# A graph network's row gathers, released five select pairs sooner

## The reference

```
gat(x):  h = x @ W                       # 4 heads of 32
         e = leaky(a_src[src] + a_dst[dst]); ex = exp(e - max over dst)
         out[dst] = sum(ex * h[src]) / sum(ex) + bias   (self loop added)
x = layernorm(x + relu(gat2(relu(gat1(x)))))
msgs = x[dst] @ Wd + x[src] @ Ws + ew * ww + bm
agg  = max of msgs over each dst (0 for a node without edges)
x = layernorm(x + relu(x @ W1a + agg @ W1b + b1) @ W2 + b2)
```

## Time and profile before

| | |
|---|---|
| median of 3 runs | 8498.15 us (8483.72 to 8513.47) |
| profiled execution, its own time | 8498.15 us |
| its span, first to last instruction | 8496.0 us |
| mean granted clock of TensorE | 0.591 of 2.4 GHz |
| busy share PE / DVE / ACT / POOL | 63 / 48 / 55 / 58% |
| 3328 gathers of layers 0 and 1, mean of one | 945 ns |
| 1664 gathers of layer 2, mean of one | 944 ns |
| moved by DMA | 943.20 MB, 111 GB/s |

### The profile page before, as it was taken

The page is one execution under the profiler, slowest core; times in us unless marked ns, Lnnn a source line. Parts: engine busy times, 40 slices in busy tenths (PEclk is TensorE's granted clock), DMA queues, the critical chain, the costliest instruction groups (busy, mean ns, idle before and its releaser), DMA issues.

```text
span 8496.0 us, 135842 instructions
## 1 busy us (share of the span) xinstructions
PE 5378.7 (63%) x24591; PEld 4960.5 (58%) x24591; DVE 4118.8 (48%) x11945; ACT 4677.6 (55%) x10649; POOL 4896.2 (58%) x5170
## 2 busy tenths in 40 slices
PE   6767776777666676676767666663555555555456
PEld 5666666666666566666666666652444444444445
DVE  3444444444445544444444444473555555555557
ACT  4656655665565565566556555572444444444447
POOL 5556666566654556566665656525566666666662
PEclk6555555555555655555555555565777777777779
DMA  7333333333332433333333333344555555555554
GB/s 196 91 95 97 95 92 97 95 94 91 96 94 64 116 100 91 95 96 94 92 96 96 94 91 97 86 138 110 138 138 134 139 139 136 137 142 135 136 142 135
DMA packets 820560, 943.20 MB, mean 111 GB/s; under 512 B 185720, under 2 KB 549570, under 8 KB 819522
## 3 DMA queue, kind: packets, MB, share of 16 engines
q1 hardware_dynamic: 658962, 595.34, 25.4%
q0 software_dynamic: 160256, 335.36, 17.8%
q10 hardware_dynamic: 432, 2.45, 0.1%
HBM read 883.19 MB, written 49.44 MB: 110 GB/s over the span
## 4 chain that ended last, share of the span: by engine, by line
PE 28%; issue 25%; DVE 20%; another core or an unknown queue 17%; DVEq 5%; ACT 2%; SPq 2%; DMA 1%; POOL 0%; ACTq 0%
PE bS L806 11%; DVE acc L1399 8%; PE bA L771 8%; PE bE L806 2%; PE bM L806 2%; DVE ch L1638 2%; DVEq L1399 2%; DVE bA L1632 2%; DVE acc L1394 2%; PE bA L694 1%; PE bE L694 1%; DVEq L1265 1%; ACT S L1054 1%; DVEq L1385 1%
## 5 line engine op out<-in xcount | busy, mean ns | idle before, releaser
L673 POOL DMA_INDIRECT G<-table,idx x3328 | 3145.5, 945 | 2141.7 <-issue 914.3
L806 PE MATMUL bS<-G,S 128*128 x8816 | 2155.1, 406 | 1032.7 <-issue 382.8
L806 PEld LDWEIGHTS bS<-G,S 128*128 128x128 f32 x8816 | 1854.5, 294 | 1146.1 <-issue 1138.2
L673 POOL DMA_INDIRECT G<-ztable,idx x1664 | 1571.4, 944 | 1013.5 <-issue 447.2
L771 PEld LDWEIGHTS bA<-adst,st 128*128 128x128 f32 x7872 | 1796.9, 331 | 434.3 <-issue 432.8
L1399 DVE TENSOR_TENSOR acc<-acc,bS 128x136 f32 (+1 forms) x4408 | 1280.7, 291 | 1587.3 <-remote 723.2
L771 PE MATMUL bA<-adst,st 128*128 x7872 | 1748.1, 344 | 333.7 <-issue 295.4
L1054 ACT ACTIVATE S<-iota_row,nd 128x128 f32<-128x128 f32 x5904 | 1864.2, 387 | 61.6 <-issue 27.2
L1040 ACT ACTIVATE st<-xr,neg_p 128x512 f32<-128x512 f32 x984 | 700.0, 711 | 1160.5 <-remote 659.7
L1058 ACT ACTIVATE S<-S,one_col 128x512 f32<-128x512 f32 x1476 | 1065.2, 722 | 68.2 <-ACT S L1054 10.0
L1044 ACT ACTIVATE st<-st,one_col 128x512 f32<-128x512 f32 x984 | 710.0, 722 | 31.9
(11 more groups left out here) (217 smaller groups left out, 4435.5 us busy)
## 6 DMA issues: line engine op xcount, KB each, us to landing
xr<-d_drel SPq DMA_DIRECT2D x984, 256.0 KB
xr<-in_ew SPq DMA_DIRECT2D x312, 256.0 KB
st<-d_neg SPq DMA_DIRECT2D x312, 256.0 KB
G<-table,idx POOLq DMA_INDIRECT x3328
G<-ztable,idx POOLq DMA_INDIRECT x1664
isend<-in_ew SPq DMA_DIRECT2D x104, 256.0 KB
isend<-d_neg SPq DMA_DIRECT2D x104, 256.0 KB
table<-G SPq DMA_DIRECT2D x48, 264.0 KB
```

What stands on the lines that cost most here:

```text
L673: pool.indirect_dma_start(G[:, r, c, 0:width], None, from_table, bass.IndirectOffsetOnAxis(ap=idx[:, r, c:c + 1], axis=0)).then_inc(gather ...
L806: mm = pe.matmul(bank_of(l, u, r, k)[:, j * w:(j + 1) * w], S[:, onehots(r, i), s, :], Gf[:, bass.ds(chunk_at[0][s], w)], start=True, stop ...
```

## The change

The constant in POOL's wait goes from + 2 to - 3: gathers c and c + 1 of batch b may start when five fewer pairs of unit b-2 are selected. For c from 0 to 5 this asks for pairs of unit b-3 only. Nothing else changes.

```diff
                     for c in range(CB):
                         if c % 2 == 0 and (not isinstance(b, int) or b >= RING):
-                            pool.wait_ge(sel_done, 2 * quad(l, b - 2, 0) + c // 2 + 2)
+                            pool.wait_ge(sel_done, 2 * quad(l, b - 2, 0) + c // 2 - 3)
                             pool.nop(nofuse=True)
```

## The result

The changed kernel takes 8576.81 us (median of 4 runs, 8574.27 to 8584.07) against 8502.58 us for the kernel before on the same chip (8483.72 to 8513.47): a ratio of 1.0091, 95% interval 1.0075 to 1.0107. It is slower by 0.9%; 8430 us was forecast. The profiled execution took 8585.75 us with a span of 8583.6 us, 87.6 us more than before.

A forecast was written before the change was run, and what follows sets the result against it. No engine was full; unpaused gather issuing by POOL was taken to hold up the other engines' hand-offs. 8498 + 0 + 0 - 94 + 24 = 8428, taken as 8430 us; range 8345 to 8590.

The forecast's parts named there:

- step 3: Rhythm of 141 batches: the three-pair threshold step moves from pairs 17 and 0 to 12 and 13; -94 and +24 us.
- layer 2, priced at 47 x +0.5 = +24 us: Layer 2: pairs 12, 13 releasing nothing joins PE's long stop, and the dense run loses its break; ends -47 and +94.
- the new hole: Place in POOL's thresholds after the change, pairs 12 and 13, which release no gathers.
- Step 1: Gathers being earlier: worth 0, since they move 14 us ahead and already have 17 us in hand.
- Step 2: Start and end of each layer: 2.6 us lost and 2.6 won, sum 0; bounds 8 us in all.
- Step 3, layers 0 and 1: Attention layers: moved pause falls in the stretch losing 12.8 us; 1.0 us gained per batch, -94 us, ends -188 and +94.
- two pauses laid on one another: Layers 0 and 1 before the change: POOL's release pause coincides with PE's 6.05 us idle before pair 0.
- The old hole: Place in POOL's thresholds before the change, pairs 17 and 0, which release no gathers.
- one long run: Rival: POOL falls behind in the dense stretch, runs of 16 gathers and more; +85 us, 8583 us; chance 0.32.
- No change: Rival: gathers cost the same wherever they fall, or layer 2 gives back the gain; 8498 within 25; chance 0.26.
- the waits don't bind: Rival: POOL's changed waits do not hold it, so nothing happens; chance under 0.02, counted with no change.
- 0.40 us per gather: Layer 0: 12.8 us between a 36.57 and a 49.40 us batch, averaged over 32 gathers, as delay to other engines' hand-offs.

The follow-up runs named there:

- not early, silent 12, 13: Against the kernel before: constant kept at + 2, thresholds two pairs later from c = 22, so pairs 12 and 13 release no gather; 8575.98 us, ratio 1.0094.
- the hole at 9, 10: Against the changed kernel: thresholds two pairs later from mid-batch; pairs 9, 10 release no gather in layers 0 and 2, pairs 3, 4 in layer 1; 8383.77 us.
- no hole: Against the kernel before: (9 * c) // 16 for c // 2, constant + 2, the 16 waits spread over 18 pairs; 8380.78 us, ratio 0.9858.
- the places 7, 8 and 9, 10 in layer 1: Two kernels, constant - 3, where those layer 1 pairs release no gather, other pairs in layers 0 and 2; 8554.84 and 8545.35 us (kernel before 8545.04).
- at 1, 2 and 3, 4 in layer 2: Two kernels, constant - 3, where those layer 2 pairs release no gather; 8468.74 us (1, 2 in all layers) and 8554.84 us (7, 8 in layer 1).

## Why the prediction was wrong

The sign was wrong through one term of step 3, **layer 2, priced at 47 x +0.5 = +24 us with ends of -47 and +94. It measured +161 us**, 3.46 us per steady batch. Two steps of it failed. The first is the place of PE's stop. I read it off one case, 8.7 us from pair 11 to pair 12, and wrote that the new hole lies "beside the stop and not in it". Over 42 batches of the same trace it is 4.5 us from pair 11 to 12, 4.0 from 12 to 13, and 9.9 from 13 to 14. The new step is over pairs 12, 13 and 14, so the longest stop of the batch lies inside it: 18.4 us for the three pairs, against 6.7 for those of the old step (17, 0, 1). The second is the price, half of what a pause in layer 0 was thought to give. What the runs showed is a wait: POOL stands until PE is through its stop, 8.13 us in the case shown and up to 10.9, and its pauses there grow by 3.3 us a batch; the gathers that it couldn't make in that time fall between pairs 1 and 8, where PE takes 7.6 us more. The change in layer 2 only shows the term by itself (8661.74 us), "not early, silent 12, 13" that it comes with the place and not with the lead (52.90 us a batch), and the hole at 9, 10, whose three pairs all come before the stop, that a hole without it need not cost anything (48.93 us, longest wait for a pair 4.4 us). A hole with the stop inside at another place than 12, 13 was not run in layer 2.

- **Step 1, earliness is worth 0:** right for the steady part, with either hole and with none. In the last batch of layers 0 and 1 it brings 8 us each.
- **Step 2, start and end 0, 2.6 us per layer either way:** too narrow. In layer 0 the undisturbed stretch before batch 5 lost 6.6 us (36.57 to 43.17), not 2.6; the last batch of layers 0 and 1 won 11.6 us each (48.1 to 36.4). And the first eight batches of layer 2 took 16 us more (442 to 458), all of it from batch 4 on, where the new waits set in; so it belongs to step 3.
- **Step 3, layers 0 and 1, 94 x -1.0 = -94 us:** right in sign, -71 measured, of which -53 are 0.54 and 0.72 us per steady batch and -18 come from the starts and ends of the layers. The change in these layers alone gave -88. The reason given was wrong. I took a hole for a pause that relieves the others, and two pauses laid on one another for one wasted. Then no hole would have been the worst. It is the best of the three in all layers: 49.34 / 49.43 / 48.88 us against 50.27 / 50.39 / 49.20. The old hole, too, had PE's stop (before pair 0, 9.4 and 9.6 us from pair 17 to it) within its three pairs and cost layers 0 and 1 about 1 us per batch; the new one costs them 0.5 us at most. That the stop inside the step is the cause there as well is argued from the same pattern, not shown: the places 7, 8 and 9, 10 in layer 1 (51.07 and 50.29) don't follow from it.
- **Range and rivals:** the time fell inside the range, near the 8583 us of "one long run". That is luck: its mechanism didn't occur as told. Between batches 8 and 50 no run is longer than 14 gathers, before or after, where 16 and more were the sign; and it was to cost all layers, while two of three gained. Only the crowding of gathers between pairs 0 and 11 is there, in layer 2. "No change" and "the waits don't bind" fell.
- **0.40 us per gather:** this is no more than the average between the two states that it was taken from. (Of the 26.66 us of POOL's wait, 22.9 lie inside the batch of 36.57.) The runs with fewer bytes and with fewer rows say that neither bytes nor rows make it, and the one with half the gathers that it isn't linear: 1.02 us for each of the second 16, with one gather after each wait, POOL's own time included. By the Trainium skill ("SBUF — State Buffer", section "Who interferes with whom") a DMA never contends with a compute engine. For the moving of data the runs agree: with 99 for 138 GB/s no change shows. The making of a gather by GpSimd is another matter, which the same section sets apart from it; so 36.57 against 49.40 us, or 32.86 against 49.20, does not speak against the rule, as the prediction has it. VectorE's 2270 instructions in layer 2's window are busy 1102.18 us with 32 gathers a batch and 1094.06 with 16: what is held up lies between its instructions, not in them.

**What stays open.** What in the issuing of a gather holds up the others; the trace only names the releasers as remote. And why the hole's cost differs by place within layers 0 and 1, and at 1, 2 and 3, 4 in layer 2.

## What to carry to other kernels

When a row of thresholds is shifted, look where its uneven step comes to lie, in every stage that shares the code: a step over three items that has the consumer's long stop inside can make the two wait in turn. Here it cost 3.5 us a batch with a stop of 9.9 us in it. Find the stop by an average over many rounds, not in one of them, and compare what the consumer takes over the items of the step (18.4 us here) with what the producer needs for what it is owed, not with a typical pause. Better, spread the steps evenly: (9 * c) // 16 for c // 2 and a wait for every gather gained 2.0% where the shift of the constant lost 0.9%.

## What was unexpected of the hardware

A gather by indirect DMA costs POOL 944 ns for 128 rows and 862 ns for 32: (944 - 862) / 96 = 0.85 ns per row, from which I estimate over 0.8 us for a gather of no rows. And what it costs the other engines didn't follow bytes or rows, but the number of gathers issued: with 16 in place of 32 per batch of layer 2, a batch fell from 49.20 to 32.86 us, which is below the 40.0 us that POOL needs to make 32, the stretches in which VectorE and ScalarE both stand went from 3.5 to 0.2 a batch, and the granted clock rose from 0.74 to 0.93 of 2.4 GHz.
